# Router logits from three bf16 parts, made one phase later in each batch

## The reference, cut to what matters

```
x = x + tanh(g_xattn) * attention_both_ways(layernorm(x), ctx)       # x, ctx: 8 batches of 512 rows of 512
xt = layernorm(x)                                                     # the rows that the router reads
logits = xt @ router_w + router_b                                     # 512 by 8 experts
gate, idx = max(softmax(logits)), argmax(softmax(logits))
x = x + tanh(g_ffn) * gate * (xt @ expert_w[idx] + expert_b[idx])     # one expert for each row
```

## Time and profile before

| what | before |
| --- | --- |
| median of 3 runs | 1246.79 us (1246.62 to 1246.98) |
| profiled execution, its own time | 1245.67 us |
| its span, first to last instruction | 1243.9 us |
| mean granted TensorE clock | 0.982 |
| busy: TensorE, DVE, ACT, POOL | 95 %, 59 %, 34 %, 27 % |
| logits' matmuls on TensorE (L899) | 256, 31.2 us |
| their copies on ACT (L997) | 32, 18.9 us |
| their reading on DVE (L1143) | 32, 5.1 us |

### The profile page before, as it was taken

How to read it: one execution, slowest core, us unless ns; L and a number is a source line. 1 busy time by engine, 2 the same in 40 slices (tenths; PEclk the granted TensorE clock), 3 DMA queues, 4 the chain that set the end, 5 groups by cost and what they waited for, 6 DMA issues and landing times.

```text
span 1243.9 us, 18325 instructions
## 1 busy us (share of the span) xinstructions
PE 1187.5 (95%) x5856; PEld 977.1 (79%) x5857; DVE 727.8 (59%) x1401; ACT 416.8 (34%) x725; POOL 334.2 (27%) x425
## 2 busy tenths in 40 slices
PE   4999999999999999999999999999999979689898
PEld 3877888888888888888888888888888857567686
DVE  2654657465746574657465746574657446866565
ACT  2333332333233323332333233323332334343342
POOL 1000043014301430143014401340134010656464
PEclk8899999999999999999999999999999989889899
DMA  5131202040205020402040203020402062364552
GB/s 166 35 102 51 68 18 102 2 51 18 95 8 51 17 85 16 51 17 84 17 51 17 84 17 51 17 84 17 49 10 90 21 91 72 118 220 103 152 147 88
DMA packets 61043, 79.39 MB, mean 64 GB/s; under 512 B 28038, under 2 KB 28038, under 8 KB 60872
## 3 DMA queue, kind: packets, MB, share of 16 engines
q1 hardware_dynamic: 48336, 59.94, 20.4%
q0 software_dynamic: 7264, 18.72, 5.0%
q10 hardware_dynamic: 5400, 0.19, 0.3%
HBM read 54.41 MB, written 26.24 MB: 65 GB/s over the span
## 4 chain that ended last, share of the span: by engine, by line
PE 87%; DMA 3%; DVE 3%; issue 2%; ACTq 1%; POOL 1%; ACT 1%; SPq 1%; POOLq 0%; DVEq 0%
PE mm L155 53%; PE u L863 14%; PE tr L820 7%; PE e_bank L155 7%; PE tr L899 2%; PE w_bank L155 2%; DMA in_tile<-in_L_ffn_expert_w 2%; ACTq L234 1%; PE e_bank L1608 1%; DMA out<-e_y,u_row 1%; DVE arena L1147 1%; DMA e_row<-x_rows_early,u_row 1%; DVE nat L321 0%; PE w_fold L372 0%; DMA normed_t<-in_L_ffn_expert_w 0%
## 5 line engine op out<-in xcount | busy, mean ns | idle before, releaser
L155 PE MATMUL mm<-arena 128*128 128x512 f32 x1536 | 372.9, 395 | 10.0 <-DVE q_pair L1050 8.6
L155 PEld LDWEIGHTS mm<-arena 128*128 128x128 f32 x1536 | 285.4, 189 | 69.9 <-DVE q_pair L1050 9.0
L863 PE MATMUL u<-pt_pair,v_pair 128*128 128x512 f32 x768 | 190.8, 397 | 0.0
L155 PE MATMUL mm<-arena,q_pair 128*128 128x512 f32 x768 | 188.9, 400 | 0.0
L155 PEld LDWEIGHTS mm<-arena,q_pair 128*128 128x128 f32 x768 | 141.5, 188 | 31.3
L863 PEld LDWEIGHTS u<-pt_pair,v_pair 128*128 128x128 f32 x768 | 139.6, 188 | 26.4
L155 PE MATMUL e_bank<-arena,e_pair 128*128 x468 | 120.8, 408 | 1.6 <-DVE e_pair L1562 1.4
L1049 DVE TENSOR_TENSOR v_pair<-mm,v_pair 128x512 fp32r<-128x512 f32 x64 | 44.2, 690 | 118.2 <-ACT v_pair L950 118.2
L1213 POOL TENSOR_SCALAR mv_x<-mv_x 128x1 f32<-128x1 f32 x32 | 13.7, 428 | 340.8 <-DVE mv_x L1111 250.4
L155 PEld LDWEIGHTS e_bank<-arena,e_pair 128*128 128x128 f32 x468 | 87.2, 193 | 20.8 <-issue 2.7
L950 ACT ACTIVATE v_pair<-mm 128x512 fp32r<-128x512 f32 x64 | 38.3, 599 | 174.2 <-PE mm L155 174.2
(11 more groups left out here) (159 smaller groups left out, 1594.9 us busy)
## 6 DMA issues: line engine op xcount, KB each, us to landing
in_tile<-in_x SPq DMA_DIRECT2D x32, 256.0 KB, 2.7
in_tile<-in_ctx SPq DMA_DIRECT2D x32, 256.0 KB, 2.8
x_tile<-in_x SPq DMA_DIRECT2D x32, 256.0 KB, 3.4
x_rows<-x_tile SPq DMA_DIRECT2D x32, 256.0 KB, 2.6
x_rows_early<-x_tile SPq DMA_DIRECT2D x28, 256.0 KB, 2.9
in_tile<-in_L_ffn_expert_w SPq DMA_DIRECT2D x27, 256.0 KB, 2.7
x_tile<-in_L_xattn_Wg SPq DMA_DIRECT2D x8, 256.0 KB, 2.7
e_bias<-in_L_ffn_expert_b SPq DMA_DIRECT2D x1, 1280.0 KB, 7.1
```

What stands on the lines that cost most here:

```text
L155: last = pe.matmul(bank, lhsT(a, c), rhs(b, c), start=start and n == 0, stop=stop and n == C * len(PASSES) - 1)
L863: last = pe.matmul(u_bank[m][:], v_pair[:, i % 2, a, tile(m)], pt_pair[:, i % 2, p], start=i == 0 and n == 0, stop=i == T - 1 and n == 2)
```

## The change

The router matrix is split once into three bf16 parts (`router_parts`), each the bf16 rounding of what the parts before left. Each tile's transposed rows are split alike: ACT copies the bank to part 0 (bf16), DVE subtracts it in place in PSUM, ACT copies the rest to part 1 (new step NR), DVE subtracts it and writes part 2 over the front of the normalised rows' buffer. LG is then 12 bf16 matmuls: row part 0 with all three router parts (24 columns), part 1 with two (16), part 2 with one (8); LR sums the three groups of 8, and RT adds the bias. NT, NR, LG and LR move from the S and V steps of d0 into its V and U steps, and the last tile's into Q of d1; RT and RK move from U of d0 into Q of d1; PT2 and PT3 go one place back. In the last batch the loads of expert chunks 3 and 4 go ahead of `store_stats`, and the EX steps shift.

```diff
@@ steps_of_a_batch
-    s += cur("S", 0, 0) + late(3) + prev("MX", 2) + prev("BS", 2) + cur("S", 0, 1) + late(4) + prev("NT", 0)
-    s += prev("MX", 3) + prev("BS", 3) + prev("NM", 2)
-    s += cur("S", 0, 2) + late(5) + prev("LG", 0) + prev("LR", 0) + prev("NT", 1) + prev("NM", 3)
-    s += cur("S", 0, 3) + cur("NP", 0, 3) + late(6) + prev("LG", 1) + prev("LR", 1) + prev("NT", 2)
-    s += prev("LR", 2) + cur("V", 0, 0) + prev("LG", 2) + prev("NT", 3) + cur("PT", 0, 0)
-    s += cur("V", 0, 1) + prev("LG", 3) + prev("LR", 3) + load(0)
-    s += cur("U", 0, 0) + cur("PT", 0, 1) + late(7, 8) + cur("V", 0, 2) + cur("PT", 0, 2) + late(9) + load(1) + cur("U", 0, 1)
-    s += prev("RT", 0) + late(10) + cur("V", 0, 3) + cur("PT", 0, 3) + load(2) + cur("U", 0, 2) + late(11)
-    s += prev("RK", 0) + cur("U", 0, 3)
+    s += cur("S", 0, 0) + late(3) + prev("MX", 2) + prev("BS", 2) + cur("S", 0, 1) + late(4)
+    s += cur("S", 0, 2) + late(5) + prev("MX", 3) + prev("BS", 3) + cur("S", 0, 3) + cur("NP", 0, 3) + late(6)
+    s += cur("V", 0, 0) + cur("PT", 0, 0) + cur("V", 0, 1) + prev("NT", 0) + load(0) + prev("NR", 0)
+    s += cur("U", 0, 0) + cur("PT", 0, 1) + late(7, 8) + prev("LG", 0) + prev("LR", 0) + prev("NM", 2)
+    s += cur("V", 0, 2) + prev("NT", 1) + late(9) + load(1) + prev("NR", 1)
+    s += cur("U", 0, 1) + cur("PT", 0, 2) + late(10) + prev("LG", 1) + prev("LR", 1) + prev("NM", 3)
+    s += cur("V", 0, 3) + prev("NT", 2) + load(2) + prev("NR", 2)
+    s += cur("U", 0, 2) + cur("PT", 0, 3) + late(11) + prev("LG", 2) + prev("LR", 2)
+    s += cur("U", 0, 3) + prev("NT", 3)
...
-    s += cur("Q", 1, 0) + late(12) + load(3) + nxt("CD", 0) + cur("Q", 1, 1) + late(13) + load(4) + nxt("CD", 1)
-    s += cur("Q", 1, 2) + late(14) + load(5) + nxt("XS", 0) + cur("Q", 1, 3) + late(15) + nxt("CT", 0) + load(6)
+    s += prev("NR", 3) + cur("Q", 1, 0) + late(12) + prev("LG", 3) + prev("LR", 3) + prev("RT", 0) + nxt("CD", 0)
+    s += cur("Q", 1, 1) + late(13) + prev("RK", 0) + load(3) + nxt("CD", 1)
+    s += cur("Q", 1, 2) + late(14) + load(4) + load(5) + nxt("XS", 0) + cur("Q", 1, 3) + late(15) + nxt("CT", 0) + load(6)
@@ steps_after
-               NM1 T1 MX2 BS2 T2 NT0 NM2 MX3 BS3 T3 LG0 LR0 NT1 NM3 T4 LG1 LR1 NT2 T5 LG2 LR2 NT3 T6 LG3 LR3 T7 RT0 T8
+               NM1 T1 MX2 BS2 T2 NT0 MX3 BS3 NR0 T3 LG0 NT1 LR0 NM2 NR1 T4 LG1 NT2 LR1 NM3 NR2 T5 LG2 NT3 LR2 NR3 T6 LG3 LR3 T7 RT0
+               T8
@@ attention_part, sync
         end_batch(B - 2)
+        for n in range(3, 5):
+            load_expert(n)
         store_stats(B - 2)
...
-        for n in range(3, 17):
+        for n in range(5, 17):
@@ attention_part, tensor
-                    pe.wait_ge(nt_copied, per_batch(bb, i))
+                    pe.wait_ge(nt_third, per_batch(bb, i))
                     for c in range(C):
-                        last = pe.matmul(of_rows[i][:, 0:E], normed_t[:, c], router_sb[:, c],
-                                         start=c == 0, stop=c == C - 1)
+                        for part in range(PARTS):
+                            n = PARTS - part
+                            last = pe.matmul(of_rows[i][:, 0:n * E], part_of_rows(i, part)[:, c],
+                                             router_parts[:, c, 0:n].rearrange("p n e -> p (n e)"),
+                                             start=c == 0 and part == 0, stop=c == C - 1 and part == PARTS - 1)
@@ attention_part, scalar: NM (i > 1), NT, NR
-                        act.wait_ge(nt_tr, per_batch(bb, i) - 2)
+                        act.wait_ge(lg_mm, per_batch(bb, i) - 2)
...
-                    act.activation(normed_t[:], bank[:].rearrange("p (c t) -> p c t", c=C),
-                                   ACT.Copy).then_inc(nt_copied, 1)
+                    act.activation(part_of_rows(i, 0), bank[:].rearrange("p (c t) -> p c t", c=C),
+                                   ACT.Copy).then_inc(nt_first, 1)
+                elif kind == "NR":
+                    act.wait_ge(nt_rest, per_batch(bb, i))
+                    act.activation(part_of_rows(i, 1), bank[:].rearrange("p (c t) -> p c t", c=C),
+                                   ACT.Copy).then_inc(nt_second, 1)
@@ attention_part, vector: NT, NR, LR, RT
+                elif kind == "NT":
+                    rows = bank[:].rearrange("p (c t) -> p c t", c=C)
+                    dve.wait_ge(nt_first, per_batch(bb, i))
+                    dve.tensor_tensor(rows, rows, part_of_rows(i, 0), ALU.subtract).then_inc(nt_rest, 1)
+                elif kind == "NR":
+                    dve.wait_ge(nt_second, per_batch(bb, i))
+                    dve.tensor_tensor(part_of_rows(i, 2), bank[:].rearrange("p (c t) -> p c t", c=C),
+                                      part_of_rows(i, 1), ALU.subtract).then_inc(nt_third, 1)
...
-                    dve.tensor_tensor(logit[:, i], bank[:, 0:E], k.router_b[:], ALU.add).then_inc(lg_read, 1)
+                    dve.reduce_sum(logit[:, i], bank[:, 0:PARTS * E].rearrange("p (n e) -> p e n", n=PARTS),
+                                   axis=AX).then_inc(lg_read, 1)
...
+                    then(dve.tensor_tensor(logit[:], logit[:], k.router_b[:].unsqueeze(1).to_broadcast([P, T, E]),
+                                           ALU.add))
```

More of the change, by code:

```diff
@@ L52 @@
 ROWX = H + 4
+PARTS = 3
 A_X, A_C, CT, XT, WV_S, WV_C, WG_C, WG_S = range(8)
@@ L203, in weights_part @@
     list_i = sb("list_i", [P, E], I32)
+    in_junk = k.junk[:].bitcast(F32)[:, 0:3 * C * E].rearrange("p (n c e) -> p n c e", n=3, c=C)
+    router_sb, router_rest = in_junk[:, 0], in_junk[:, 1:3]
     rank_i = sb("rank_i", [P, T, E], I32)
@@ L215, in weights_part @@
     nat_hi, nat_lo, wide_made = sem("nat_hi"), sem("nat_lo"), sem("wide_made")
+    router_split = sem("router_split")
     group_mm, group_hi, group_lo = sem("w_group_mm"), sem("w_group_hi"), sem("w_group_lo")
@@ L321, in split, with split_router @@
             dve.tensor_tensor(nat[:, j % 2, LO], raw[:, j], f32(nat[:, j % 2, HI]), ALU.subtract).then_inc(nat_lo, 1)
+        def split_router():
+            rest = router_sb
+            for part in range(PARTS):
+                dve.tensor_copy(k.router_parts[:, :, part], rest).then_inc(router_split, 1)
+                dve.wait_ge(router_split, 2 * part + 1)
+                if part < PARTS - 1:
+                    dve.tensor_tensor(router_rest[:, part], rest, k.router_parts[:, :, part],
+                                      ALU.subtract).then_inc(router_split, 1)
+                    dve.wait_ge(router_split, 2 * part + 2)
+                    rest = router_rest[:, part]
         dve.wait_ge(b_loaded, 16 * 4)
@@ L341, in run @@
                 dve.wait_ge(scalars_ready, 2)
+                if d == 0:
+                    split_router()
                 if d == 1:
@@ L385, in run @@
                     pe.wait_ge(fold_read, 2)
+                    pe.wait_ge(router_split, 2 * PARTS - 1)
         return run
@@ L504, in attention_part @@
     normed = sb("normed", [P, H])
-    normed_t = sb("normed_t", [P, C, P])
+    normed_t = sb("normed_t", [P, 2, C, P], BF16)
     bn_1 = sb("bn_1", [P, 6])
@@ L522, in attention_part, with part_of_rows @@
     slot_i = sb("slot_i", [P, T], I32)
+    def part_of_rows(i, part):
+        if part < 2:
+            return normed_t[:, part]
+        return (normed, diff)[i % 2][:, 0:H // 2].bitcast(BF16).rearrange("p (c t) -> p c t", c=C)
     mm_bank = [ps("mm0"), ps("mm1")]
@@ L539, in attention_part @@
     tanh_done, diff_ready, diff_used, mix_done = sem("tanh_done"), sem("diff_ready"), sem("diff_used"), sem("mix_done")
-    nt_copied, x1_done, x1_stats, normed_ready = sem("nt_copied"), sem("x1_done"), sem("x1_stats"), sem("normed_ready")
+    nt_first, nt_rest, nt_second, nt_third = (sem(n) for n in ("nt_first", "nt_rest", "nt_second", "nt_third"))
+    x1_done, x1_stats, normed_ready = sem("x1_done"), sem("x1_stats"), sem("normed_ready")
     x_scaled, x1_scaled = sem("x_scaled"), sem("x1_scaled")
@@ L606, in take @@
             kind, rel, d, i = step
-            if kind == "LR":
+            if kind in ("NR", "LR"):
                 return self.of_rows[i]
@@ L1276, in attention_part @@
     return part
-DVE_LINKS = 45
+DVE_LINKS = 46
 POOL_LINKS = 24
@@ L1338, in experts_part @@
     starts_ready, experts_ready = sem("starts_ready"), sem("experts_ready")
-    early_idx_loaded = [sem(f"early_idx_loaded{i}") for i in range(EARLY)]
+    early_idx_loaded = [sem(f"early_idx_loaded{i}") for i in range(EARLY // 2)]
     idx_in_loaded = [sem(f"idx_in_loaded{i}") for i in range(TURN)]
@@ L1402, in gather @@
             if early:
-                await_count(pool, waits_passed, early_idx_loaded[tile], 16)
+                await_count(pool, waits_passed, early_idx_loaded[tile // 2], 32)
                 idx, rows = early_idx[:, tile:tile + 1], x1_early
@@ L1440, in run @@
             elif kind == "IW":
-                for n in range(EARLY):
```

(3 more changed lines are left out.)

10 lines of the change are left out of this document (5 added, 5 removed).

## The result

The changed kernel takes 1274.25 us (median of 4 runs, 1269.82 to 1286.32) where the kernel before takes 1246.79: a ratio of 1.0236, 95 % interval 1.0162 to 1.0309. The forecast was 1260.5 with a range to 1274.0: slower, as forecast, but +27.5 us, twice the +13.7. The profiled execution of after took 1271.29 us, its span 1269.5; the span of before was 1243.9.

A forecast was written before the change was run, and what follows sets the result against it. TensorE, busy for 95 % of the span, was taken to bound the kernel. Terms -16.1 + 9.8 + 6.0 + 3.2 + 5.4 + 6.7 - 1.3 gave +13.7 us: median 1260.5 us, range 1243 to 1274.

The forecast's parts named there:

- past the queues: Work after the later gate: statistics stores hold SyncE's queue and delay C2, 5.4 us in six batches; POOL's scatters cost 0.
- C2: Load behind the stores on SyncE, wanted by TensorE's transposes: 0.9 us late per batch, 5.4 in six, bounds 0 and 30.
- the tail: After the last batch: cheaper logits gain 1.6 us, LG0's chain waits behind MX3 and BS3; net -1.3, bounds -2 and +1.5.
- The logits' products: Router logits on TensorE: 12 bf16 matmuls cost 0.40 us per tile, gaining 2.30 per batch, 16.1 in seven.
- U(0,3): Product in d0 that waits for PT(0,3)'s low part from ACT and DVE: 1.22 us per batch, 9.8 in eight.
- S(0,3) and PT(0,0): Steps of d0 that wait for Exp and scaled rows once NT and LG leave: 0.85 us per batch, 6.0 in seven.
- LG3: Last tile's logits, in Q of d1, wait for their third part behind U3's subtractions on DVE: 3.2 us in seven batches.
- The last batch: S(1,0) idles 13.2 us for expert load EX5 behind the stores, against 8.60 before: +6.7 us, bounds -7.4 and +8.
- The sum: All terms over the whole kernel: +13.7 us, giving a span of 1257.6 and a median of 1260.5.
- case of the faster kind: Whole kernel measurably faster than before, chiefly if loads behind the stores land promptly (1241 us); chance of faster 0.12.
- rival 4: Router logits: bf16 pairs no cheaper than fp32, a loss of 8.3 us in place of 16.1 gained, 1285 us; chance 0.04.
- rival 3: C2 lands as late as in the middle batch's row: up to 30 us in place of 5.4, 1268 to 1285; chance 0.15.

The follow-up runs named there:

- e2: Changed kernel with the PT(0,3) transposes moved ahead of product U(0,2): 1257.94 us, 1.0096 of the kernel before.
- e4: Kernel before the change with the two statistics stores issued from ScalarE's queue instead of SyncE's: 1242.66 us, ratio 0.9964.
- e7: Changed kernel with PT(0,3) ahead of U(0,2), stores on ScalarE, last batch's stores behind S(1,3), token-list loads later: 1247.26 us, 1.0009 of before.
- e9: Changed kernel with POOL's scatters issued behind the Exp of S(1,3), stores still on SyncE: 1253.57 us, 1.0058 of the kernel before.
- e10: Kernel before the change with its scatters issued behind the Exp of S(1,3), stores where they were: 1240.56 us, ratio 0.9936.
- e3: Changed kernel with the two statistics stores issued from ScalarE's queue instead of SyncE's: 1252.65 us, 1.0051 of the kernel before.
- e1: Changed kernel run again, unaltered: 1268.88 us, one run.
- e13: Changed kernel without the last batch's four scatters, list loads starting when the places are known: 1271.67 us, one run.
- e16: Changed kernel with NR0 ahead of MX3 and BS3 on VectorE after the last batch: 1278.25 us, one run.
- e14: Kernel before the change without the last batch's four scatters, list loads starting when the places are known: 1240.12 us, one run.
- e11: Changed kernel with PT(0,3) ahead of U(0,2), stores on ScalarE, and in the last batch scatters behind S(1,3)'s Exp: 1235.47 us, 0.9900 of before.

## Why the prediction was wrong in size, step by step

The direction was right. One step had the cause wrong (past the queues: the stores were blamed, the scatters put at 0), and three terms were mis-sized: the logits' gain (16.1 us forecast, about 9 measured), C2 (5.4 forecast, 7.8 measured) and the tail (-1.3 forecast, +6.7 measured).

- **The logits' products.** New price right: 0.28 and 0.09 behind it, 0.37 for the forecast 0.40. The gain of 2.30 per batch was too high. A batch grew by 0.68 and holds 1.13 (U3), 0.33 (LG3) and about 0.47 (PT0, S3) of waits, so the rest fell by only 1.25: of the 3.90 that the step put down to the fp32 logits, 0.74 was called "a wait and dearer neighbours", with no row for what would end it. Another 0.3 is lost at the eight gate products, 2.79 us each for 2.75, for which I found no cause. Four products at 0.79 in place of four at 0.37, less that 0.3, would be 1.4, so by this sum next to none of the 0.74 went; which neighbour keeps it no run shows. Over 7 batches 7 us less gain than forecast.
- **U(0,3).** 1.1 each, 8.9 in 8 batches, where 1.22 and 9.8 stood. Right, and shown by e2.
- **S(0,3) and PT(0,0); LG3.** 0.9 and 2.4 us in all for 6.0; 2.3 for 3.2. Right in place, too high. These and U3 make up for 4 to 5 of the 7.
- **Past the queues.** This is the step that failed in its cause. It said that the stores hold SyncE's queue and that POOL's four scatters cost 0. e4, e7, e9 and e10 show the scatters slowing the loads beside them (6.1 to 13.1 us for 2.4 to 3.0), with no store ahead of these loads; and with the scatters moved, C2 is not waited for, though the stores stand where they stood (e9). The trace of before already had it, in its DMA view of 996.3 to 1013:

```profile
in_tile<-in_L_ffn_expert_w SPq DMA_DIRECT2D x3, 256.0 KB, 13.2
token_lists<-token_ids,slot_i POOLq DMA_INDIRECT x4, 13.0
x_rows_early<-stats SPq DMA_DIRECT2D x1, 8.0 KB, 3.1
```

The second store, issued at 996.35, had landed 12.4 us before the load of the earlier trace rows; the scatters landed as late as the loads. The 13.04 was read as the time behind a store, because the store is what stands ahead of it in the queue; the scatters, issued at the same moment on another engine, are in no line of that chain. What stands ahead in SyncE's queue is not nothing either: with stores and residual loads away and the scatters in place C2 was in time (e3). So C2's wait took both, the scatters and what stood ahead in the queue. Its size, 5.4, is near the 5.6 of waits in the profiled execution by luck: not 0.9 in each batch but 0.7, 1.1 and 3.8 in three, and 6.2, 13.5 and 10.9 in other executions. Against steps of 125.71 these three cost 7.8, since the clock falls behind the longest. This may also make the 16 us between the runs of after; only one of them has a trace, so that is not shown.
- **The last batch.** +6.7 forecast, +6.8 measured (+4.7 in e1), 13.2 of idle time for 12.9, EX5 the load that ends it. Right in number in the profiled execution, since the same scatters stood beside the same loads, but the cause was only in part the one given: the idle time is 9.2 to 12.9 in four executions of this order (after, e1, e13, e16), 5.6 are left without the scatters (e9), and those go with EX5's place behind the gate, the stores and the residual loads. The 8.60 of before was the scatters': e10.
- **The tail.** The largest miss: -1.3 forecast, +6.7 in the profiled execution, +3.6 in the next. Two parts. The chain is 2.8 longer without any scatter (e13 and e14, one execution each), where the step had counted the saved logits (1.6) as a gain; TensorE stands waiting for gathers in that stretch, so I read it that shorter logits are worth nothing there, which no run tests alone. The remaining 0.2 to 3.9 comes and goes with the scatters, and TensorE waits there for the experts' rows; how the scatters hold these gathers is argued, not shown. Why they cost more in after's order than in before's, beyond that they come 2.6 to 2.9 us later after the last batch, stays open.
- **The sum.** In the profiled spans +25.6 for +13.7: 8.0 from the tail, 3.8 from the batches, 0.1 from the last one. The median lies 3 above the profiled execution.

The chances had the direction right: no case of the faster kind came true, and rival 4 (dear bf16 pairs) fell on the first row of LG. The median lies inside rival 3's 1268 to 1285 by luck: that rival put up to 30 us on C2, which cost 7.8 in the traced execution.

## What to carry to other kernels

When a load lands late, look at what every queue has under way in that stretch, not only at what stands ahead of it in its own, and look when that neighbour itself landed; here the chain named the queue's neighbour, not the disturber. Move the suspected small transfers one kind at a time, and see what else an edit lets go sooner. In this kernel the scatters of single words belong in a stretch whose loads have slack. And where a product gets cheaper but needs a longer chain through other engines, give that chain a whole product of cover (U(0,2), 2.75 us, over PT(0,3)'s chain of 1.4 ended the wait in e2), and keep each step's old neighbours ahead of it (PT(0,3) ahead of U(0,2)).

## What the runs showed of the hardware

- Four scatters of 128 single words take 19.0 (e7, e9) to 21.2 us (after) from the first issue until POOL goes on behind the last landing, and in that time a 256 KB load on SyncE's queue takes 6.1 to 13.1 us in place of 2.4 to 3.0, with no store ahead of it (e3, e4, e7, e9). What in the scatters does it, their single words or their queue, no run separates. Of two stores of 8 KB in 16-byte pieces, 1056 packets, the second lands in 2.0 to 3.1 us (e9, e10); loads beside them on another queue take 2.7 to 2.8 (e11), loads behind them and two residual loads on the same queue 4.1 to 6.0 (e9, e10). The Trainium skill (DMA: Bandwidth & Descriptors, Specifications) has one threshold for both, 512 bytes; here pieces of 16 bytes and scattered ones of 4 behave differently.
- With the stores on ScalarE's queue and SyncE no longer stopped at the gate, C2 was never waited for (e3), where it had been for 5.5 to 13.5 us in all (after, e1, e2, e13, e16).
- After a wait of 3.77 us TensorE's next product took 4.59 us at a granted clock of 0.58 (after).
- A bf16 weight load with its matmul of 8 to 24 columns takes 0.023 us in a row of 12.
